# The row numbers move from the row one-hots to the expert and block one-hots, with the order of the routing stage rearranged

## The reference

```python
x = x + tanh(g_xattn[0]) * L0_xattn(layernorm(x), ctx, ctx)       # 64 keys per batch
x = x + tanh(g_ffn[0]) * L0_ffn(layernorm(x))                     # 16 experts, the best 2 per row
x = x + tanh(g_xattn[1]) * L1_xattn(layernorm(x), ctx)            # x @ W1.T + mean(ctx) @ W2.T + b
x = x + tanh(g_ffn[1]) * L1_ffn(layernorm(x))                     # 256 -> 1024 -> 1024 -> 1024 -> 256
# L0_ffn
scores = softmax(x @ gate_w); topk_w, topk_idx = top_k(scores, 2); topk_w /= sum(topk_w)
h = silu(x @ w1[e]) * (x @ w3[e]);  y = sum over the 2 experts of topk_w * (h @ w2[e]);  return y + x
```

## Time and profile before

| | us |
|---|---|
| median of three runs | 497.9 (496.54 to 498.03) |
| the profiled execution, its time | 501.49 |
| its span | 499.6 |
| busy: PE / DVE / ACT / POOL | 474.8 / 316.6 / 217.9 / 149.0 |
| TensorE's granted clock, mean | 0.993 of full speed |

### The profile page before, as it was taken

The page is one execution under the profiler, slowest core; times in us unless marked ns, Lnnn a source line. Parts: engine busy times, 40 slices in busy tenths (PEclk is TensorE's granted clock), DMA queues, the critical chain, the costliest instruction groups (busy, mean ns, idle before and its releaser), DMA issues.

```text
span 499.6 us, 7859 instructions
## 1 busy us (share of the span) xinstructions
PE 474.8 (95%) x2760; PEld 409.5 (82%) x2760; DVE 316.6 (63%) x848; ACT 217.9 (44%) x444; POOL 149.0 (30%) x157
## 2 busy tenths in 40 slices
PE   6988979997698999999999999999999999999996
PEld 6877869997697788888978888887888898788886
DVE  2888897876675865765477766337865735554523
ACT  1679936775466966412372121336121224511110
POOL 2487857767860601110350201053110101000000
PEclk8999999999999999999999999999999999999999
DMA  8784834897653587212140420032122002022101
GB/s 285 253 284 141 284 121 142 235 315 231 203 168 114 169 288 240 76 30 77 43 128 21 106 63 2 0 101 69 43 85 64 1 1 84 15 71 69 38 2 48
DMA packets 34465, 58.82 MB, mean 118 GB/s; under 512 B 4529, under 2 KB 18353, under 8 KB 34354
## 3 DMA queue, kind: packets, MB, share of 16 engines
q1 hardware_dynamic: 29760, 47.12, 29.3%
q0 software_dynamic: 3840, 10.49, 7.3%
q10 hardware_dynamic: 818, 0.61, 0.4%
HBM read 47.85 MB, written 14.42 MB: 125 GB/s over the span
## 4 chain that ended last, share of the span: by engine, by line
PE 79%; DVE 7%; DMA 5%; POOL 5%; issue 2%; ACT 0%; ACTq 0%; DVEq 0%; POOLq 0%
PE bank L2017 23%; PE bank L2018 23%; PE bank L1986 6%; PE bank L1989 6%; PE bank L2050 3%; PE bank L2049 3%; PE bank L1594 2%; PE bank L1596 2%; PE bank L1595 2%; DMA xg<-xb_dram,perm 2%; POOL y_first L629 2%; POOL xg_more L648 1%; POOL xg L648 1%; DMA colv<-cols 1%; PE bank L1831 1%
## 5 line engine op out<-in xcount | busy, mean ns | idle before, releaser
L1568 ACT ACTIVATE sg<-bank,colv 128x512 f32<-128x512 f32 x64 | 44.1, 690 | 176.6 <-PE bank L2018 176.6
L2017 PE MATMUL bank<-Ah,Wr 128*128 128x512 f32 x256 | 100.2, 391 | 0.0
L2017 PE MATMUL bank<-Bh,Wr 128*128 128x512 f32 x256 | 99.9, 390 | 0.0
L2018 PE MATMUL bank<-Al,Wr 128*128 128x512 f32 x256 | 99.8, 390 | 0.0
L2018 PE MATMUL bank<-Bl,Wr 128*128 128x512 f32 x256 | 99.7, 389 | 0.0
L2017 PEld LDWEIGHTS bank<-Ah,Wr 128*128 128x128 f32 x256 | 48.1, 188 | 11.2 <-DVE Al L1281 0.8
L2018 PEld LDWEIGHTS bank<-Bl,Wr 128*128 128x128 f32 x256 | 48.1, 188 | 9.8
L2017 PEld LDWEIGHTS bank<-Bh,Wr 128*128 128x128 f32 x256 | 48.1, 188 | 9.8
L2018 PEld LDWEIGHTS bank<-Al,Wr 128*128 128x128 f32 x256 | 48.1, 188 | 9.7
L1294 DVE CAST Ah<-sg 128x512 fp32r<-128x512 f32 x32 | 13.6, 425 | 60.0 <-ACT sg L1568 60.0
L1594 PE MATMUL bank<-EL,turned 128*128 (+1 forms) x137 | 42.6, 311 | 0.3 <-ACT yb L1500 0.3
(11 more groups left out here) (294 smaller groups left out, 1024.8 us busy)
## 6 DMA issues: line engine op xcount, KB each, us to landing
Wraw<-panels SPq DMA_DIRECT2D x44, 256.0 KB, 3.8
stage<-panels SPq DMA_DIRECT2D x44, 256.0 KB, 2.6
ES<-experts SPq DMA_DIRECT2D x16, 384.0 KB, 5.2
ys_dram<-yb SPq DMA_DIRECT2D x47, 128.0 KB
ys_dram<-x SPq DMA_DIRECT2D x1, 1920.0 KB, 7.9
X<-x SPq DMA_DIRECT2D x3, 512.0 KB, 7.6
xb_dram<-xb SPq DMA_DIRECT2D x3, 512.0 KB, 5.2
out<-outb SPq DMA_DIRECT2D x3, 512.0 KB, 3.3
```

Of the source, the lines that this page charges most:

```text
L1568: eng.activation(sg[:, (8 * layer + m) % 3, :], bank[m % 4][:, :], ACT.Gelu, scale=colv[:, c + m:c + m + 1]).then_inc(f_act[m], 1)
L2017: mm(bank[m % 4][:, :], Wr[:, base:base + P], h[0][:, k, :], start=k == 0, stop=False)
L2018: ins = mm(bank[m % 4][:, :], Wr[:, base:base + P], h[1][:, k, :], start=False, stop=k == FK - 1 and not general)
```

## The change

The row numbers are multiplied into the narrow one-hots. GpSimd makes `eqt` = `eq` x `tok1` for each group (`tokens_of`), and `first_hot` reads it in place of `eq`; VectorE multiplies `ohb` by `tok16` in two more instructions. `ohr` stays a plain one-hot: `tokens_in` of ScalarE is gone, and group 3's eight scalar instructions become two `tensor_tensor` of 512 columns.

The ranks get bank 3 of their own, and `rank_picked` no longer waits for the next logits. `row_products` moves from group 2 to group 3 (into bank 5), `context_rows` behind the ranks and counts of group 3, and ScalarE's `nm1` and `w3s` behind `rows_normed` of group 3. ScalarE makes one expert in group 2 instead of three, and the last three after `crow` and `ex`. GpSimd cuts an expert's low part in four, and the last half of expert 12 moves behind gather 4. In group 3 `mean2` is made by VectorE, whose rows go by mean and rstd. The fill of `ys_dram` is issued in two halves after experts 10 and 11, and VectorE's rows are stored ahead of ScalarE's. `low(0)` and `low(1)` move into VectorE's chain, `experts_of_blocks` behind it into the block loop, and the second permutation behind `gate_up(1)`. The first three blocks have their own rounded rows.

```diff
--- before.py
+++ after.py
@@ -52,10 +52,14 @@
+FILL_AT = (10, 11)
+LOW_AT = 4
-EL_CUT = 2
+EL_CUT = 4
+RANK_FILLERS = (0, 2, 4, 4)
@@ -239,7 +243,8 @@
-        eq = put("eq", [P, NG, TOPK, TG, E], F16)
+        eq, eqt = put("eq", [P, NG, TOPK, TG, E], F16), put("eqt", [P, TOPK, TG, E], F16)
+        tok16 = put("tok16", [P, NT], F16)
@@ -343,9 +350,11 @@
+        bank_ranks, bank_places, bank_late = bank[3], bank[1], bank[5]
         def turned_pair(n):
-            return (first_high[n], first_low[n]) if n < 2 else (t_high[n % 3], t_low[n % 3])
+            return (first_high[n], first_low[n]) if n < FIRST else (t_high[n % 3], t_low[n % 3])
@@ -397,8 +406,7 @@
         def ranks_of(g):
-            first = TG * SC + (TG * E if g == NG - 1 else 0)
-            return bank[(g + 1) % 2][:, first:first + TG * E]
+            return bank_ranks[:, 0:TG * E]
@@ -445,18 +453,21 @@
+                if e in FILL_AT:
+                    n = T * TOPK - E * P
+                    a, b = (n * (FILL_AT.index(e) + k) // len(FILL_AT) for k in range(2))
+                    eng.dma_start(ys_dram[E * P + a:E * P + b, :], x[a:b, :]).then_inc(dma_fill, 16)
-            eng.dma_start(ys_dram[E * P:T * TOPK, :], x[0:T * TOPK - E * P, :]).then_inc(dma_fill, 16)
-            store_rows(NG - 1, 0, 2)
-            eng.wait_ge(dma_fill, 32)
+            store_rows(NG - 1, 0, 2)
+            eng.wait_ge(dma_fill, 16 + 16 * len(FILL_AT))
@@ -548,10 +559,13 @@
-                own(eng.tensor_scalar(mean2[:, ts], mv2[:, ts, 0], -1.0, None, ALU.mult))
+                if g < NG - 1:
+                    own(eng.tensor_scalar(mean2[:, ts], mv2[:, ts, 0], -1.0, None, ALU.mult))
+                if g == NG - 1:
+                    eng.wait_ge(dve_mean, 1)
@@ -580,6 +594,7 @@
             def split_low(n):
+                n = n * EL_CUT // 2
@@ -589,6 +604,17 @@
+            def tokens_of(g):
+                if g == 0:
+                    eng.wait_ge(act_rep, 2)
+                else:
+                    eng.wait_ge(dve_ohf, g)
+                eng.wait_ge(dve_both, g + 1)
+                eng.tensor_tensor(eqt[:, :, :, :], eq[:, g, :, :, :],
+                                  tok1[:, g * TG:(g + 1) * TG].unsqueeze(1).unsqueeze(3).to_broadcast([P, TOPK, TG, E]),
+                                  ALU.mult).then_inc(pool_eqt, 1)
@@ -602,13 +628,11 @@
+                tokens_of(g)
-                else:
-                    eng.wait_ge(dve_both, NG)
-            split_low(2)
@@ -650,6 +674,8 @@
+                if i == LOW_AT:
+                    split_low(2)
@@ -851,9 +877,6 @@
-                if g + 1 < NG:
-                    eng.wait_ge(pe_lg, g + 2)
@@ -870,18 +893,22 @@
             def first_hot(g):
+                eng.wait_ge(pool_eqt, g + 1)
-                                         eq[:, g, :, :, :].rearrange("p r t e -> p (r t) e"), ALU.is_lt, ALU.mult).then_inc(dve_ohf, 1)
+                                         eqt[:, :, :, :].rearrange("p r t e -> p (r t) e"), ALU.is_lt, ALU.mult).then_inc(dve_ohf, 1)
             def rows_normed():
-                eng.wait_ge(pool_fac, NG)
+                eng.wait_ge(ln_var[1], NG)
+                ts = slice((NG - 1) * TG, NT)
+                eng.tensor_scalar(mean2[:, ts], mv2[:, ts, 0], -1.0, None, ALU.mult).then_inc(dve_mean, 1)
+                eng.wait_ge(ln_rstd[1], NG)
-                    eng.tensor_scalar(xb[:, 1, j, :], X[:, t, :], rstd2[:, t:t + 1], nmr2[:, t:t + 1],
-                                      ALU.mult, ALU.add).then_inc(dve_xb, 1)
+                    eng.tensor_scalar(xb[:, 1, j, :], X[:, t, :], mv2[:, t, 0:1], rstd2[:, t:t + 1],
+                                      ALU.subtract, ALU.mult).then_inc(dve_xb, 1)
@@ -894,15 +921,11 @@
-                for j in range(TG):
-                    for r in range(TOPK):
-                        t = g * TG + j
-                        ins = eng.tensor_scalar(ohr[:, g, j, r, :], krow[:, :], pos[:, g, r, j:j + 1], tok1[:, t:t + 1],
-                                                ALU.is_equal, ALU.mult)
-                        if (j, r) == (TG - 1, TOPK - 1) or (j, r) == (TG // 2 - 1, TOPK - 1):
-                            ins.then_inc(dve_ohr, 1)
-                        else:
-                            own(ins)
+                for q in range(2):
+                    js, _ = halves(q)
+                    eng.tensor_tensor(ohr[:, g, js, :, :], krow[:, :].unsqueeze(1).unsqueeze(1).to_broadcast([P, 2, TOPK, P]),
+                                      pos[:, g, :, js].rearrange("p r t -> p t r").unsqueeze(3).to_broadcast([P, 2, TOPK, P]),
+                                      ALU.is_equal).then_inc(dve_ohr, 1)
@@ -972,7 +995,7 @@
-            permuted(bank[3], slice(0, E))
+            permuted(bank_places, slice(0, E))
@@ -998,6 +1021,12 @@
+            def low(n):
+                b, w = n % 3, joint(n)
+                high_, low_ = turned_pair(n)
+                eng.wait_ge(b_xh, n + 1)
+                eng.tensor_tensor(low_[:, w], bank_t[b][:, w], high_[:, w].bitcast(F32), ALU.subtract).then_inc(b_xl, 1)
@@ -1009,11 +1038,13 @@
+            low(0)
+            low(1)
@@ -1021,12 +1052,34 @@
-            eng.wait_ge(act_rep, 3)
+            eng.wait_ge(act_rep, 4)
-                eng.tensor_tensor(ohb[:, r, :, :], kbrep[:, :, :],
-                                  pblk16[:, r, :].unsqueeze(1).to_broadcast([P, NREST, NT]), ALU.is_equal).then_inc(dve_ohb, 1)
+                own(eng.tensor_tensor(ohb[:, r, :, :], kbrep[:, :, :],
+                                      pblk16[:, r, :].unsqueeze(1).to_broadcast([P, NREST, NT]), ALU.is_equal))
+            own.done()
+            for r in range(TOPK):
+                eng.tensor_tensor(ohb[:, r, :, :], ohb[:, r, :, :],
+                                  tok16[:, :].unsqueeze(1).to_broadcast([P, NREST, NT]), ALU.mult).then_inc(dve_ohb, 1)
+            def experts_of_blocks():
+                own(eng.tensor_scalar(bexp[:, :], pinc_0[:, :], 1.0 / P, kc[:, K_TOK:K_TOK + 1], ALU.mult, ALU.is_le))
...
@@ -1154,25 +1201,6 @@
-            low(0)
...
-            low(1)
@@ -1183,6 +1211,7 @@
+                    experts_of_blocks()
@@ -1391,13 +1420,6 @@
-            def tokens_in(g):
-                eng.wait_ge(dve_ohr, g + 1)
-                for j in range(TG):
-                    eng.activation(ohr[:, g, j, :, :], ohr[:, g, j, :, :], ACT.Copy,
-                                   scale=tok1[:, g * TG + j:g * TG + j + 1]).then_inc(act_ohr, 1)
@@ -1459,20 +1481,20 @@
+                    eng.wait_ge(act_rep, 2)
+                    eng.activation(tok16[:, :], tok1[:, :], ACT.Copy).then_inc(act_rep, 1)
-                    tokens_in(g - 1)
-                if g == 2:
-                    eng.wait_ge(pe_setup, PE_LATE)
-                    eng.activation(nm1[:, :], bank[3][:, 0:D], ACT.Copy, scale=-1.0 / D).then_inc(act_setup, 1)
-                    eng.activation(w3s[:, :], bank[3][:, D:2 * D], ACT.Copy, scale=tg[:, 3:4]).then_inc(act_setup, 1)
-                    split_high(3)
+                    split_high(3 if g < NG - 2 else 1)
-            split_high(E)
+            split_high(1)
+            eng.wait_ge(pe_setup, PE_LATE)
+            eng.activation(nm1[:, :], bank_late[:, 0:D], ACT.Copy, scale=-1.0 / D).then_inc(act_setup, 1)
+            eng.activation(w3s[:, :], bank_late[:, D:2 * D], ACT.Copy, scale=tg[:, 3:4]).then_inc(act_setup, 1)
@@ -1616,6 +1638,8 @@
+                if k == 0 and g > 2:
+                    eng.wait_ge(dve_rk, g - 2)
@@ -1691,9 +1715,10 @@
             def ranks(g):
+                eng.wait_ge(act_xT, DK * min(NG, g + 3))
-                   start=False, stop=False, skip_group_check=True)
+                   start=True, stop=False, skip_group_check=True)
@@ -1717,10 +1742,10 @@
-                eng.wait_ge(act_xT, DK * NG)
+                eng.wait_ge(act_x1, 2 * (NG - 1))
-                    mm(bank[3][:, 0:D], ones128[:, :], W1s[:, k, :], start=k == 0, stop=k == DK - 1)
-                mm(bank[3][:, D:2 * D], ones[:, :], rowv[:, R_S3:R_S3 + D], start=True, stop=True).then_inc(pe_setup, 1)
+                    mm(bank_late[:, 0:D], ones128[:, :], W1s[:, k, :], start=k == 0, stop=k == DK - 1)
+                mm(bank_late[:, D:2 * D], ones[:, :], rowv[:, R_S3:R_S3 + D], start=True, stop=True).then_inc(pe_setup, 1)
@@ -1761,14 +1786,11 @@
-                if g == 2:
-                    row_products()
-                if g == NG - 1:
-                    context_rows()
-                    keep_clock(bank[2], 5)
+                    row_products()
+                keep_clock(bank[2], RANK_FILLERS[g])
@@ -1783,6 +1805,8 @@
+            context_rows()
@@ -1794,17 +1818,15 @@
             def first_there(r, t):
-                    eng.wait_ge(act_setup, ACT_LATE + 1)
-                    keep_clock(bank[5], 6)
-                    eng.wait_ge(act_ohr, TG * (NG - 1))
+                    eng.wait_ge(dve_ohr, NG - 1)
```

(11 more changed lines are left out.)

40 lines of the change are left out of this document (18 added, 22 removed).

## The result

The kernel before took 497.82 us and the changed kernel 501.51 us (medians of eight runs each): ratio 1.0089, 95% interval 1.0066 to 1.0112; the two medians alone divide to 1.0074. So it is slower by 3.7 us (medians) to 4.4 us (ratio). The profiled execution of after has a span of 504.3 us against 499.6, and it is the slowest of its eight. The forecast was 500.3, slower, in a range of 495.4 to 503.2.

A forecast was written before the change was run, and what follows sets the result against it. Bound: the routing groups, paced by VectorE, then the chain through the first gather to the third expert block. Terms +0.1 - 1.0 + 1.75 + 1.6 = +2.45 us on the median 497.9 gave 500.3 us, range 495.4 to 503.2.

The forecast's parts named there:

- C: From the first gather to the third expert block: VectorE's new order makes that block later by 1.75 us.
- D: Expert 12's pieces behind gather 4 meet four VectorE operations before the third block: +1.6 us, 0 if they miss.
- term B: From GpSimd's last `nmr` to the first gather, set by ScalarE's path: -1.0 us, between -1.4 and -0.9.
- A: The four routing groups, up to GpSimd's last `nmr`: waits removed, but 12 port meetings cost 5.9 us; net +0.1 us.
- rival 3: In the routing groups, GpSimd becomes the bound: +3.0 us there, kernel at 503.2 us; chance 0.12.
- 1 (pieces seldom meet): In the groups and behind gather 4, GpSimd's short pieces seldom meet VectorE: 495.8 us; chance 0.22.
- 2 (cancel): Gains and costs from the groups to the third block cancel, with eight or nine meetings: 497.9 us; chance 0.28.
- 4: Before the first gather, the stores' best landing sets it, not ScalarE's last experts: 498.7 us; no chance of its own.
- No port rule: In the groups and behind gather 4, no meeting of GpSimd and VectorE costs anything: 492.9 us; given no chance.
- held operations: Sign in the groups: VectorE's ixf, eq, pos, both and one-hots take 0.5 to 0.7 us beside a GpSimd piece.
- The last row store: Sign ahead of the first gather: the last store of normalised rows lands within 3 us.
- VectorE idle for 2 to 3 us before low(0): Sign between the first gather and the third block: VectorE stops for 2 to 3 us, waiting to start low(0).

The follow-up runs named there:

- cut2: Changed kernel with GpSimd's low halves cut in two pieces (128x384) instead of four (128x192); 502.57 us, ratio to the kernel before 1.0087.
- order_cut2: `order_back` with GpSimd's low halves cut in two pieces instead of four; ratio to the kernel before 1.0067, on the second chip.
- order_act: `order_back` with ScalarE's last three experts put ahead of `nm`, `w3s`, `crow` and `ex`; ratio to the kernel before 0.9998, on the second chip.
- fill_right_2: Changed kernel with 13 more clock fillers in TensorE's first idle stretch, 3 and 5 at two other places; 501.38 us, ratio to the kernel before 1.0079.
- after_again: Changed kernel run again unaltered, on the third chip beside `fill_right_2`; 503.35 us, ratio to the kernel before 1.0133.
- order_back: Changed kernel with low(0) and low(1) put back behind the block one-hots, the 32 products ahead of the first block's; 499.99 us, ratio 1.0029.
- tokens_alone: Kernel before with only the token move into `eqt` and `ohb`; bank, order, cut and fill untouched; ratio to the kernel before 1.0033, second chip.

## Why the prediction was right, point by point

The sign, the time (501.5 for 500.3) and the range held, and with them the sum C + D and term B. A was missed, and one cause was not in the account at all. The forecast's own range, 499.4 to 501.4, was just missed; the wide one held because it reached up to rival 3. The order, the largest cost, was priced about right; part of the rest is luck, as the points say.

- **A, +0.1; measured +1.03.** Its parts: the wait of `rtmp` went, as said. The blocked time, 12 x 0.49 = 5.9 us forecast, is 5.8 us in six rows. That is luck: I had 12 meetings of 0.49, and it is 17 of 0.34 on average, so that two errors cancel. The step that failed is the price of a piece: "halved, to about 0.49", measured 0.56 to 0.62, and with it the assumption that VectorE sets the end of the groups. VectorE was 0.5 us earlier than before; GpSimd's queue made it late. A second part of that lateness was not in the account: the `veps` that VectorE held, 1.06 us in each of two groups. GpSimd as the bound is rival 3's mechanism, which I had given 0.12, at a third of its price (+3.0). `cut2` and `order_cut2` support it: fewer pieces, `nmr` 0.8 earlier, though `cut2` was no faster for it.
- **B, -1.0; measured 6.34 us from nmr to the gather against 7.39, -1.05.** The releaser is ScalarE's last EH, and `order_act` shows by how much it holds the gather (1.15). The row tiles took 0.38 each (0.75 for two). Right for its reason.
- **The clock; not in the sum, measured +1.06.** From the gather to low(0) it is 4.77 us against 3.71. "TensorE has time there, since it fills the wait for the last one-hots with clock fillers" was the sentence that missed it. I counted the fillers that hid work and not those that the change takes out of TensorE's queue ahead of the gather: behind the permutation 18 rows (2.25 us) became 8 (1.14), and TensorE's wait there went from 0.95 to 3.25 us. `fill_right_2` against `after_again`: low(0) 1.3 us earlier with the clock at 1.00. But this term does not simply add to the next ones: with low(0) on time the pieces hold more of the chain, and 1.1 of the 1.3 us were gone at the 32 products.
- **C and D, +3.35 together; measured 8.10 - 4.95 = +3.15.** The 32 products start 4.89 us behind low(0), between the 3.8 without meetings and the 5.4 with four. Three held operations cost 0.9 us, not 1.6, because the one-hots themselves came after the last piece: gather 4 was done 1.2 us behind low(0) and not 2.3, since low(0) was late and the gathers were not. So D is 0.9 and C the rest, 2.2 for 1.75; that the sum fits so well is luck. Where low(0) is not late, in `fill_right_2`, the products start 5.67 behind it, which is D's case (5.4). Behind them it is 3.2 us to the third block and not 2.9, in part at half clock. `order_back` shows the order as the cause: -2.66 us at the third block, -3.65 at the end.
- **The sum.** 1.03 - 1.05 + 1.06 + 3.15 = 4.19 at the third block, 4.93 at the end of the profile, about 4.4 by the ratio; 2.45 was forecast. As a sum of stretches, the miss up to the third block's first product is A (0.9) and the clock (1.1); the next 0.7 us lie in the third block itself, where the clock was at half (80 to 86 us): 1.66 us from its first product to its `bsg` against 1.00.
- **Rivals.** 1 (pieces seldom meet) and 2 (cancel) did not come: the meetings did. 4 is inside B and went against it. "No port rule" is refuted by the rows of VectorE.
- **What would show it.** `rtmp` no wait, held operations 0.46 to 0.66, row tiles at 0.4, first gather by EH: all seen. The last row store landed in 3.2 us, a little over the 3. "VectorE idle for 2 to 3 us before low(0)": it was 5.1, since low(0) came late and the new order left VectorE nothing else.

## What to carry to other kernels

A piece of work cut in two costs more than two halves: count the added instructions on the engine that runs them, and ask whether that engine becomes the one without a pause. When two engines share a port, look at the busy share of both, since the slow one may now end the stage though the fast one is early. When a change takes work out of TensorE's queue or moves its fillers, go through its idle stretches as for any other wait. And do not stop an idle engine in the middle of its list for a result that is 5 us away, when the rest of the list is due behind it: by `order_back` that order cost more here (3.65 us of 4.93 at the end of the profiles) than all else together. And do not expect a stage's gain to pass on: here an earlier low(0) only met more of GpSimd's pieces.

## What the runs showed of the hardware

- GpSimd's two-input product: 128x384 in 0.97 to 1.0 us, 128x192 in 0.56, 128x128 (16 bit) in 0.40. By the first two I estimate 0.15 us of each as independent of the size. Over the changed kernel's 52 pieces the mean was 0.62.
- A held operation of VectorE can wait for more than the piece in course: 2.55 us over two pieces back to back (`cut2`), 2.66 (`order_cut2`), 1.48 over three of the short ones (`order_back`). In `cut2` it had been issued half a microsecond ahead of the first piece, while GpSimd's span is that of the gather; why it did not pass there is open. `ecol_0` in `order_back` (0.59) was held in the same place. A gather alone does not do it: in the kernel before, `pslot` at 71.16 took 0.18 us beside the gather of 70.41 to 71.35.
The Trainium skill, SBUF — State Buffer, section "Who interferes with whom", says that whoever issues first gets the shared pair of ports for the whole instruction, and that the other is blocked. The rows of single meetings agree (0.46 to 0.66 us); the 2.55 us over two instructions are more than that sentence gives.
- The holding is mutual: beside VectorE's row one-hots GpSimd's `rstd` took 2.07 us instead of 1.04 (`tokens_alone`) and its `veps` 1.29 instead of 0.23 (the changed kernel).
- With TensorE idle from 65.6 to 68.8 us its granted clock was 0.50 for most of the next ten fillers, which then took 4.1 us instead of 2.5 on the path: fillers that are meant to keep the clock, placed behind the wait, lengthened it.
